# Scale of the context from a sum on TensorE, VectorE's side work moved behind the first score maxima: one change to a fused kernel of attention and experts

## The chip, the cores and the metric

The kernel runs on one core of a Trainium2 chip. A core has five engines that work side by side and meet through semaphores: TensorE (PE; its weight loads are shown as PEld), VectorE (DVE), ScalarE (ACT), GpSimd (POOL) and SyncE (SP), which here only issues DMAs. Each engine takes its instructions in the order in which the program lists them, so an instruction that waits holds back everything behind it on its engine. The metric is the device time of one execution in microseconds.

## The reference

For 64 batches of 256 rows with 1024 columns (`x`) and a context of 256 rows with 256 columns each, attention with 32 query heads on 8 key heads is added to `x`, and then a mixture of 8 experts, two for each row:

```python
x = x + attention(layernorm(x), ctx_512, ctx_512)       # 32 heads of 32, 8 key heads
x = x + experts(layernorm(x), router_w, w1, w2)         # top 2 of 8, inner width 704
# attention: softmax(q k^T / sqrt(32)) v, keys and values are both the context
# experts:   logits = x router_w^T; top 2; softmax of the two;
#            y = w2[e] (silu(gate) * up), gate and up from w1[e] x
```

All is in fp32; the kernel computes it with pairs of fp16 numbers, a high part and a low part, and for that scales each operand by a power of two that is found from its largest absolute value.

## The kernel before

The program has stages one after another: constants and the split of the weights into high and low parts (to 420 us), the stage `fuse` (to about 8730 us), and two stages that run the rest of the expert blocks of 512 and 256 rows. The change is in `fuse` alone.

`fuse` runs iterations i = 0 to 67. Iteration i loads batch i, scales and splits its context (iterations 0 to 63), computes score maxima for batch i - 1 and exponentials and values for the batches before it, adds attention to x and normalizes for batch i - 3, routes batch i - 4, and from i = 13 on it multiplies one block of 512 rows with an expert's weights. From iteration 14 on pairs of iterations are the body of a hardware loop, up to 61; every engine has its own copy of it and jumps back to its head every second iteration. An iteration has eight steps, k = 0 to 7, and a step four quarters, q = 0 to 3. In each step TensorE multiplies four score tiles (L704) and four tiles for the maxima (L721), adds up the values (L686 to L690), and between them, in 64 even pieces per iteration, the experts' products (L862, L883). This interleaving is written out by hand, in the `iteration` function of each engine; there is no planner.

What moves one step forward goes through all engines: the scores of L704 lie in one PSUM tile, `a_sc`. ScalarE reads it twice (L946 to `a_p` in fp32, L947 to `a_ph` in fp16). The fp16 rest `a_pl` = `a_p` - `a_ph` is made by GpSimd for the quarters 0 and 1 (L1172) and by VectorE for 2 and 3 (L1364). `a_p` has one buffer for each quarter, so ScalarE cannot write quarter 0 or 1 of the next step before GpSimd has read that of the last. VectorE divides the values (L1373, L1376, to `a_att`), and may write the next `a_att` when GpSimd has added the last to `a_xres` (L1145). VectorE's maxima of the scores (L1343) free the two halves of `a_mx` for TensorE.

The scale of the context: at step 0, VectorE takes the largest absolute value in each partition (`largest_ctx`, L1418, to `a_cmax`). GpSimd makes one maximum of the 128, in all partitions (`partition_all_reduce`, L1193, to `a_call`). At step 1 VectorE makes the power of two and its inverse from it (`scale_ctx`, L1424 to L1431), with which ScalarE and VectorE split the context into `a_ksrc`.

What stands around these in the order of each engine: on GpSimd the all-reduce stands between the subtraction of quarter 0 and that of quarter 1 in step 0, followed by the DMA that adds the experts' last rows to the output (`add_rows`, L1132). On VectorE step 0 begins with `largest_ctx` and `pick_block` (L1315 to L1334, eleven small instructions that choose the next block of rows and its expert), then come the copies of the turned queries (`q_out`, L1357), the first score maxima (`max_out`, L1343) and the attention output (`o_out`). In steps 1 and 2, the statistics of the next x (`stats_x`, L1396) stand ahead of these too. `a_mi` is one PSUM bank in which TensorE puts small things: the turned maxima (`turn_max`, L810), logits and counts.

Of the kernel before, what the change touches and what calls it, by code (L numbers as in the profile page):

```python
# [5 lines left out]
P = 128  # L6
# [12 lines left out]
D = 32  # L19
# [325 lines left out]
def fuse(nc, x, ctx_in, x1, xn_parts, slots, w1_parts, w2_parts, scales, router_parts, router_scale, ident,  # L345
# [29 lines left out]
    with ExitStack() as ctx:  # L375
        def sb(name, shape, dt):
            return ctx.enter_context(nc.sbuf_tensor(name, shape, dt))
# [26 lines left out]
        nb1, nb2 = sb("a_nb1", [P, 2], F32), sb("a_nb2", [P, 2], F32)  # L404
        cmax, call, cgrd = sb("a_cmax", [P, 1], F32), sb("a_call", [P, 1], F32), sb("a_cgrd", [P, 1], F32)
        cpow, crec, cinv = sb("a_cpow", [P, 1], F32), sb("a_crec", [P, 1], F32), sb("a_cinv", [P, 1], F32)
# [40 lines left out]
        LG = MI[:, 256:256 + 2 * E].rearrange("p (c e) -> p c e", c=2)  # L447
        CN = MI[:, 320:320 + 3 * E].rearrange("p (c e) -> p c e", c=3)
        Y = ps("e_y", [P, 2, BLOCK], F32)

# [217 lines left out]
        def _(pe):  # L668
            pe.wait_ge(filled, 2)
            pe.wait_ge(rows_cleared, 3)  # L670
# [109 lines left out]
            def turn_rows(i, g):  # L780
# [16 lines left out]
                last.then_inc(turned, 1)  # L797

            def turn_max(i, k):
                b, p = mtu(i, k - 1)  # L800
                if k % 2 == 0 or not on(b):
                    return
                pe.wait_ge(n["maxed"], b * 32 + 8 * (p + 1))
                at_least(pe, n["max_low"], b * 4 + p)
                if k == 5 and on(i - 4):
                    pe.wait_ge(n["route"], (i - 4) * ROUTE + 1)
                if k == 7 and on(i - 4):
                    pe.wait_ge(n["route"], (i - 4) * ROUTE + COUNTS_READ)
                for c in range(2):
                    last = pe.transpose(MI[0:2 * G, c * P:(c + 1) * P], nmax[:, c, 8 * p:8 * p + 8], ident[:, :])  # L810
                last.then_inc(n["max_turned"], 1)
# [88 lines left out]
            def iteration(i, par, fused):  # L900
                for k in range(8):
# [14 lines left out]
                    max_score(i, k, par, 2)  # L916
                    turn_max(i, k)
                    values(i, k, par)
                    experts(i, 8 * k + 5, par, fused)
# [11 lines left out]
        def _(act):  # L931
            act.wait_ge(filled, 2)

# [158 lines left out]
        def _(pool):  # L1092
            pool.memset(xg[:, :, :].rearrange("p a b -> p (a b)").bitcast(U32), 0).then_inc(xg_cleared, 1)
            pool.memset(ksrc[:, :, :, 3 * D:3 * D + 2], 1.0).then_inc(filled, 1)
            pool.memset(ksrc[:, :, :, 3 * D + 2:P], 0.0).then_inc(filled, 1)
# [88 lines left out]
            def iteration(i, par, fused):  # L1184
                m, m1 = i - LAG, i - LAG + 1
                now, soon, before = live(m, fused), live(m1, fused), live(m - 1, fused)
                for k in range(8):
                    low_p(i, k, 0)
                    if k == 0 and on(i):
                        pool.wait_ge(n["ctx_max"], i + 1)  # L1190
                        at_least(pool, n["ctx_chain"], i * 4)
                        settle(pool, passed)
                        pool.partition_all_reduce(call[:, :], cmax[:, :], P, RMAX).then_inc(n["ctx_all"], 1)  # L1193
                    if k == 0 and before:
# [39 lines left out]
        def _(dve):  # L1234
# [186 lines left out]
            def scale_ctx(i):  # L1421
                dve.wait_ge(n["ctx_all"], i + 1)
                at_least(dve, n["k_low"], i)
                dve.tensor_scalar(cgrd[:, :], call[:, :], 1e-30, None, ALU.max).then_inc(n["ctx_chain"], 1)  # L1424
                dve.wait_ge(n["ctx_chain"], i * 4 + 1)
                dve.tensor_single_scalar(cpow[:, :].bitcast(I32), cgrd[:, :].bitcast(I32), EXPONENT,
                                         ALU.bitwise_and).then_inc(n["ctx_chain"], 1)
                dve.wait_ge(n["ctx_chain"], i * 4 + 2)
                dve.reciprocal(crec[:, :], cpow[:, :]).then_inc(n["ctx_chain"], 1)
                dve.wait_ge(n["ctx_chain"], i * 4 + 3)  # L1430
                dve.tensor_scalar(cinv[:, :], crec[:, :], 8.0, None, ALU.mult).then_inc(n["ctx_chain"], 1)  # L1431

# [9 lines left out]
            def scale_exps(i, par):  # L1442
                at_least(dve, n["exps"], (i - 1) * 32)
                dve.tensor_scalar(escale[:, par:par + 1], cpow[:, :], 0.125 / float(D) ** 0.5, None,
                                  ALU.mult).then_inc(n["escaled"], 1)

            def scale_values(i, par):
                dve.tensor_scalar(vscale[:, par:par + 1], cpow[:, :], 0.125, None, ALU.mult).then_inc(n["vscaled"], 1)

# [81 lines left out]
            def iteration(i, par, fused):  # L1531
                for k in range(8):
                    if k == 0 and on(i):
                        largest_ctx(i, par)
                    if k == 0 and live(i - LAG + 1, fused):
                        pick_block(i - LAG + 1, par)
                    if k in (1, 2) and on(i):
                        stats_x(i, k - 1)
                    q_out(i, k)
                    if k == 1 and on(i - 3):  # L1540
                        spread_x1(i - 3)
                    experts(i, 8 * k, par, fused)
                    max_out(i, k, 0)
                    o_out(i, k, par)
                    if k == 5 and on(i - 4):
# [512 lines left out]
```

## Time and profile before

| | us |
|---|---|
| median of three executions | 10104.24 (10095.11 to 10106.83) |
| the profiled execution | 10093.03 |
| its span, first to last instruction | 10091.3 |
| mean granted clock of TensorE | 0.913 |
| TensorE busy | 8676.8 (86%) |
| VectorE busy | 6024.0 (60%) |
| ScalarE busy | 4560.9 (45%) |
| GpSimd busy | 3786.1 (38%) |

The profile is of one execution. Its waits view sums, for each engine, tile and line, the idle time just before an instruction, by the instruction that released it; "issue" as the releaser means that no semaphore is seen to have held it. A windows row gives, for a stretch in us, its length, then busy time and count of instructions of PE, PEld, DVE, ACT and POOL, the granted clock of TensorE as a share of full speed (1.00 is 2.4 GHz, 0.50 is 1.2 GHz), the share of DMA and GB/s. A timeline row has start, length, engine, line, operation, tiles, shapes, count, and in brackets the idle time before it with its releaser. The row of a line gives the least, median and largest duration in ns.

### The profile page before, as it was taken

Reading aid. Unit: us, or ns where it says so; the run is one execution under the profiler, and the core shown is the slowest. Engines: PE = TensorE matmul, PEld = TensorE weight load, DVE = VectorE, ACT = ScalarE, POOL = GpSimd, SP = SyncE. Lnnn points to the kernel's source line nnn. Section 1 sums busy time; section 2 is a strip of 40 time slices with the busy share of each in tenths; the row PEclk is TensorE's granted clock in tenths of the full one; section 3 lists DMA queues with packets and bytes.
Section 4 is the critical chain, followed back from the end, with each engine's and each line's share of the span. In section 5 each row is a group of like instructions: output and inputs, shape, how many; then the busy total and the mean of one; then the engine's idle time right before and its main releaser. Section 6 shows DMA issues by size and latency. Waiting matters only on the chain. (4 is left out here: it accounts for less than half of the span.)

```text
span 10091.3 us, 212936 instructions
## 1 busy us (share of the span) xinstructions
PE 8676.8 (86%) x73448; PEld 4865.3 (48%) x73448; DVE 6024.0 (60%) x11995; ACT 4560.9 (45%) x6962; POOL 3786.1 (38%) x5045
## 2 busy tenths in 40 slices
PE   4455569999898999999999899999989989989989
PEld 3333335544444555555455445545545545444457
DVE  7877776666666666666666666666666666222212
ACT  3466654554544555554455544445554445200001
POOL 0145544444444444444444444444444444211111
PEclk7656569999999999999999999999999999999999
DMA  9742124444444444444444444444444444454444
GB/s 366 299 167 96 46 86 137 132 126 128 127 135 131 135 124 134 129 131 135 131 137 123 131 123 136 136 133 132 125 129 128 135 131 138 124 191 146 157 168 165
DMA packets 455392, 1434.12 MB, mean 142 GB/s; under 512 B 90088, under 2 KB 110568, under 8 KB 454128
## 3 DMA queue, kind: packets, MB, share of 16 engines
q1 hardware_dynamic: 360240, 1132.12, 33.3%
q0 software_dynamic: 94016, 287.65, 12.2%
q8 instruction: 615, 10.08, 0.4%
q14 instruction: 521, 4.27, 0.1%
HBM read 1034.41 MB, written 408.21 MB: 143 GB/s over the span
## 5 line engine op out<-in xcount | busy, mean ns | idle before, releaser
L862 PE MATMUL e_y<-e_xt,e_w 128*128 128x512 f16 x14520 | 3601.7, 387 | 0.0
L946 ACT ACTIVATE a_p<-a_sc,a_escale 128x512 f32<-128x512 f32 x2048 | 1407.1, 687 | 3026.2 <-PE a_sc L704 2202.4
L1172 POOL TENSOR_TENSOR a_pl<-a_p,a_ph 128x512 f16<-128x512 f32 x1024 | 1232.9, 1204 | 3008.2 <-ACT a_ph L947 2429.9
L1343 DVE TENSOR_REDUCE a_nmax<-a_mx 128x2 f32<-128x512 f32 x2048 | 1404.9, 687 | 1218.2 <-PE a_mx L721 1201.8
L862 PEld LDWEIGHTS e_y<-e_xt,e_w 128*128 128x128 f16 x14520 | 1391.2, 99 | 1412.0 <-issue 96.7
L883 PE MATMUL e_y<-e_w,e_yt 128*128 128x512 f16 x7480 | 1863.6, 379 | 41.1 <-DVE e_yt L1506 41.1
L704 PE MATMUL a_sc<-a_qs,a_ks 128*128 128x512 f16 x2048 | 854.6, 417 | 845.0 <-ACT a_ph L947 817.1
L947 ACT ACTIVATE a_ph<-a_sc,a_escale 128x512 f16<-128x512 f32 x2048 | 1395.2, 681 | 0.0
L883 PEld LDWEIGHTS e_y<-e_w,e_yt 128*128 128x128 f16 x7480 | 695.4, 97 | 697.3 <-issue 65.0
L721 PE MATMUL a_mx<-a_ks,a_qs 96*128 96x256 f16 x4096 | 865.9, 296 | 143.2 <-DVE a_nmax L1343 139.1
L704 PEld LDWEIGHTS a_sc<-a_qs,a_ks 128*128 128x128 f16 x2048 | 203.7, 99 | 1178.4 <-ACT a_ph L947 866.5
L1364 DVE TENSOR_TENSOR a_pl<-a_p,a_ph 128x512 f16<-128x512 f32 x1024 | 758.3, 741 | 14.4 <-ACT a_ph L947 14.2
L1357 DVE COPY a_qs<-a_tr 64x1024 f16<-64x1024 f16 (+1 forms) x1024 | 701.5, 685 | 59.9 <-PE a_tr L743 47.4
L721 PEld LDWEIGHTS a_mx<-a_ks,a_qs 96*128 96x128 f16 x4096 | 413.4, 104 | 625.9 <-DVE a_nmax L1343 169.7
L686 PE MATMUL a_pv<-a_v,a_ph 128*128 128x34 f16 x8192 | 693.0, 182 | 6.9 <-DVE a_att L1376 4.4
L690 PE MATMUL a_pv<-a_v,a_pl 128*128 128x34 f16 x8192 | 687.1, 181 | 0.0
L688 PE MATMUL a_pv<-a_v,a_ph 128*128 128x32 f16 x8192 | 686.7, 180 | 0.0
L686 PEld LDWEIGHTS a_pv<-a_v,a_ph 128*128 128x128 f16 x8192 | 658.4, 99 | 48.1 <-DVE a_att L1376 23.5
L688 PEld LDWEIGHTS a_pv<-a_v,a_ph 128*128 128x128 f16 x8192 | 650.5, 99 | 10.4
L690 PEld LDWEIGHTS a_pv<-a_v,a_pl 128*128 128x128 f16 x8192 | 645.1, 99 | 0.0
L1036 ACT ACTIVATE e_rows<-e_y,e_gate 128x512 f32<-128x512 f32 x440 | 302.4, 687 | 587.3 <-PE e_y L883 420.9
L1145 POOL TENSOR_TENSOR a_xres<-a_att,a_xres 128x128 f32<-128x128 f32 x1024 | 524.9, 563 | 38.7 <-DVE a_att L1376 36.2
(236 smaller groups left out, 11485.3 us busy)
## 6 DMA issues: line engine op xcount, KB each, us to landing
e_w<-w_parts SPq DMA_DIRECT2D x935, 512.0 KB, 3.5
f_w<-w_parts SPq DMA_DIRECT2D x153, 512.0 KB, 5.2
w_parts<-w_parts SPq DMA_DIRECT2D x136, 512.0 KB, 4.9
h_w<-w_parts SPq DMA_DIRECT2D x136, 512.0 KB, 6.1
a_x<-in_x SPq DMA_DIRECT2D x64, 1024.0 KB, 4.9
a_xres<-in_x SPq DMA_DIRECT2D x64, 1024.0 KB, 8.1
out<-a_xres SPq DMA_DIRECT2D x64, 1024.0 KB, 7.7
xn_parts<-a_xhl SPq DMA_DIRECT2D x64, 1024.0 KB, 10.0
```

Source lines behind the costliest of these rows:

```text
L686: pe.matmul(PV[:, c, g, 0:D + 2], PH[:, kv % 2, g // 2, tt, cols], V1[:, vp, tt, kv, 0:D + 2], start=tt == 0, stop=False)
L688: pe.matmul(PV[:, c, g, 0:D], PH[:, kv % 2, g // 2, tt, cols], V1[:, vp, tt, kv, D + 2:2 * D + 2], start=False, stop=False)
L690: last = pe.matmul(PV[:, c, g, 0:D + 2], PL[:, kv % 2, g // 2, tt, cols], V1[:, vp, tt, kv, 0:D + 2], start=False, stop=tt == 1)
L704: pe.matmul(SC[:, :], KS[:, sp_, kv, tt * P:(tt + 1) * P], QS[:, kv, half * 2 * S:(half + 1) * 2 * S], start=True, stop=True).then_inc(n[" ...
L721: last = pe.matmul(MX[:, q % 2, g2, :], QS[0:96, kv, g * S + half * P:g * S + half * P + P], KS[0:96, mp, kv, :], start=True, stop=True)
L862: last = pe.matmul(Y[:, bank, :], w1r[:, t % RING, h, pw, :], xT[:, px, h, :], start=r == 0, stop=r == 3 * HT - 1)
L883: last = pe.matmul(Y[:, bank, :], yT[:, py, t, c * P:(c + 1) * P], w2b[:, t, pw, half * (H // 2):(half + 1) * (H // 2)], start=r == 0, sto ...
L946: act.activation(PF[:, q, :], SC[:, :], ACT.Exp, scale=escale[:, sp_:sp_ + 1])
L947: act.activation(PH[:, kv % 2, h, tt, :], SC[:, :], ACT.Exp, scale=escale[:, sp_:sp_ + 1]).then_inc(n["exps"], 1)
L1172: pool.tensor_tensor(PL[:, kv % 2, q // 2, q % 2, :], PF[:, q, :], PH[:, kv % 2, q // 2, q % 2, :], ALU.subtract).then_inc(n["p_low"], 1)
L1343: dve.reduce_max(nmax[:, half, kv * G + 2 * gp:kv * G + 2 * gp + 2], MX[:, q % 2, :, :], AX.X, negate=True).then_inc(n["maxed"], 1)
L1364: dve.tensor_tensor(PL[:, kv % 2, q // 2, q % 2, :], PF[:, q, :], PH[:, kv % 2, q // 2, q % 2, :], ALU.subtract).then_inc(p_low2, 1)
```

## The change

The maximum over partitions becomes a sum over partitions: TensorE multiplies a matrix of ones in fp32 with the column of the 128 maxima (`sum_ctx`), in step 0 behind the third pair of matmuls for the score maxima and ahead of the values. The sum, in all 128 partitions, lies in one column of `a_mi`, from which `scale_ctx` reads it. The sum is between 1 and 128 times the largest value, so the constants change: 1024 in place of 8, and 2^-10 in place of 0.125. The matrix of ones is written once by GpSimd at the stage's start. The turn of the maxima in step 1, which writes to the same PSUM bank, waits until the sum has been read. On VectorE, `q_out`, the experts' instructions of the step's first piece, `max_out` of quarter 0 and `o_out` now come ahead of `largest_ctx`, `pick_block` and `stats_x`.

```diff
         CN = MI[:, 320:320 + 3 * E].rearrange("p (c e) -> p c e", c=3)
+        CS = MI[:, 352:353]
...
+            def sum_ctx(i):
+                if not on(i):
+                    return
+                pe.wait_ge(n["ctx_max"], i + 1)
+                at_least(pe, n["max_low"], (i - 2) * 4 + 3)
+                pe.matmul(CS, ones[:, :], cmax[:, :], start=True, stop=True).then_inc(n["ctx_all"], 1)
+
             def turn_max(i, k):
                 b, p = mtu(i, k - 1)
                 if k % 2 == 0 or not on(b):
                     return
+                if k == 1 and on(i):
+                    pe.wait_ge(n["ctx_chain"], i * 4 + 1)
...
                     turn_max(i, k)
+                    if k == 0:
+                        sum_ctx(i)
                     values(i, k, par)
...
                     low_p(i, k, 0)
-                    if k == 0 and on(i):
-                        pool.wait_ge(n["ctx_max"], i + 1)
-                        at_least(pool, n["ctx_chain"], i * 4)
-                        settle(pool, passed)
-                        pool.partition_all_reduce(call[:, :], cmax[:, :], P, RMAX).then_inc(n["ctx_all"], 1)
                     if k == 0 and before:
                         add_rows(m - 1, par, 3)
...
-                dve.tensor_scalar(cgrd[:, :], call[:, :], 1e-30, None, ALU.max).then_inc(n["ctx_chain"], 1)
+                dve.tensor_scalar(cgrd[:, :], CS, 1e-30, None, ALU.max).then_inc(n["ctx_chain"], 1)
...
                 for k in range(8):
+                    q_out(i, k)
+                    if k == 1 and on(i - 3):
+                        spread_x1(i - 3)
+                    experts(i, 8 * k, par, fused)
+                    max_out(i, k, 0)
+                    o_out(i, k, par)
                     if k == 0 and on(i):
                         largest_ctx(i, par)
                     if k == 0 and live(i - LAG + 1, fused):
                         pick_block(i - LAG + 1, par)
                     if k in (1, 2) and on(i):
                         stats_x(i, k - 1)
-                    q_out(i, k)
-                    if k == 1 and on(i - 3):
-                        spread_x1(i - 3)
-                    experts(i, 8 * k, par, fused)
-                    max_out(i, k, 0)
-                    o_out(i, k, par)
```

GpSimd in the loop, at the turn from step 0's first subtraction to its second (`a_pl`); the ISA rows without a tile at L1193 and L1172 are those that the trace shows as MODIFY_POOL_CONFIG. Before:

```order
L1172 TENSOR_TENSOR a_pl<-a_p,a_ph 128x512 [waits a_exps]
L1190 REGISTER_ALU
L32 REGISTER_ALU [waits a_ctx_max]
L1193 ISA [waits a_ctx_chain]
L1193 ISA a_call<-a_cmax 128x1
L1126 REGISTER_ALU
L1132 DMA out<-e_rows,e_idx 16384x1024 [waits e_weighed]
L1171 REGISTER_ALU
L1172 ISA
L1172 TENSOR_TENSOR a_pl<-a_p,a_ph 128x512 [waits a_exps]
L1142 REGISTER_ALU
L1145 TENSOR_TENSOR a_xres<-a_att,a_xres 128x128 [waits a_o_done]
```

After:

```order
L1185 TENSOR_TENSOR a_pl<-a_p,a_ph 128x512 [waits a_exps]
L1139 REGISTER_ALU
L1145 DMA out<-e_rows,e_idx 16384x1024 [waits e_weighed]
L1184 REGISTER_ALU
L1185 TENSOR_TENSOR a_pl<-a_p,a_ph 128x512 [waits a_exps]
L1155 REGISTER_ALU
L1158 TENSOR_TENSOR a_xres<-a_att,a_xres 128x128 [waits a_o_done]
```

The reduction and the two MODIFY_POOL_CONFIG rows are gone; between the subtractions stands only the DMA that adds rows.

VectorE in the loop, from the last routing instruction of the iteration (`tok`) into step 0. Before:

```order
L1307 TENSOR_SCALAR tok<-tok 128x2 [waits a_route]
L1418 TENSOR_REDUCE a_cmax<-a_ctx 128x1 [waits a_ctx_all,ctx_in1]
L1312 REGISTER_ALU
L32 ISA [waits a_route]
L1315 TENSOR_TENSOR e_left<-next_slot,taken 128x8 [waits e_y1_there,e_picked]
...
L1334 CAST e_blk<-e_spot 128x1 [waits e_picked]
L1357 COPY a_qs<-a_tr 64x4x256 [waits a_scores,a_q_turned]
L1357 COPY a_qs<-a_tr 32x4x256
L1357 COPY a_qs<-a_tr 64x4x256
L1357 COPY a_qs<-a_tr 32x4x256
L1340 REGISTER_ALU
L1343 TENSOR_REDUCE a_nmax<-a_mx 128x2 [waits a_max_turned,a_max_scores]
```

After:

```order
L1315 TENSOR_SCALAR tok<-tok 128x2 [waits a_route]
L1365 COPY a_qs<-a_tr 64x4x256 [waits a_scores,a_q_turned]
L1365 COPY a_qs<-a_tr 32x4x256
L1365 COPY a_qs<-a_tr 64x4x256
L1365 COPY a_qs<-a_tr 32x4x256
L1348 REGISTER_ALU
L1351 TENSOR_REDUCE a_nmax<-a_mx 128x2 [waits a_max_turned,a_max_scores]
L1379 REGISTER_ALU
L32 REGISTER_ALU [waits a_pv]
L1381 RECIPROCAL a_orec<-a_pv 128x8 [waits a_x1_done]
L1384 SCALAR_TENSOR_TENSOR a_att<-a_pv,a_vscale,a_orec 128x256 [waits a_vscaled,a_o_recip]
L1426 TENSOR_REDUCE a_cmax<-a_ctx 128x1 [waits a_ctx_all,ctx_in1]
...
L1323 TENSOR_TENSOR e_left<-next_slot,taken 128x8 [waits e_y1_there,e_picked]
```

The copies to `a_qs`, the maxima `a_nmax` and the output `a_att` have moved ahead of the context's maximum and of the picking of a block, which begins with `e_left`.

TensorE in the loop, step 0, from the third pair of matmuls for the maxima to the values (`a_pv`), after the change:

```order
L722 MATMUL a_mx<-a_ks,a_qs 128x256 [waits a_maxed]
L722 MATMUL a_mx<-a_ks,a_qs 128x256
L803 REGISTER_ALU
L32 REGISTER_ALU [waits a_ctx_max]
L805 MATMUL a_mi<-a_cmax,a_ones 128x1 [waits a_max_low]
L679 ISA
L32 ISA [waits a_v_made,a_p_low2,a_p_low]
L687 MATMUL a_pv<-a_v,a_ph 128x34 [waits a_o_done]
L689 MATMUL a_pv<-a_v,a_ph 128x32
```

The matmul of L805 and its waits are new, ahead of the values; the other rows stand as before.

## Rows read from the trace of the kernel before

**Rows 1.** Waits, 1736.72 to 8276.70: total us, times, longest us.

```profile
ACT a_p L946 <- POOL a_pl L1172: 590.8, 48, 17.0
DVE a_orec L1373 <- POOL a_xres L1145: 507.3, 48, 14.6
...
POOL a_pl L1172 <- issue: 475.4, 57, 10.9
PE a_sc L704 <- ACT a_ph L947: 449.3, 59, 13.9
...
POOL a_call L1193 <- issue: 338.3, 48, 9.0
...
DVE a_cmax L1418 <- issue: 114.7, 23, 6.0
...
PE a_mx L721 <- DVE a_nmax L1343: 81.5, 23, 4.1
```

**Rows 2.** Windows view of the same stretch.

```profile
1736.72:8276.70 6539.98, 5945.00 (x52082) 3294.36 (x52081) 4175.04 (x8593) 3294.64 (x4993) 2787.98 (x3696) 0.95 0.45 131
```

**Rows 3.** Windows view of one pair of iterations, in pieces.

```profile
5006.09:5025.70 19.61, 19.59 (x145) 10.14 (x143) 17.88 (x41) 8.76 (x14) 10.04 (x12) 1.00 0.86 240
5025.70:5037.90 12.20, 0.02 (x1) 0.02 (x2) 0.47 (x2) 1.26 (x2) 2.79 (x5) 0.65 0.43 86
5037.90:5043.20 5.30, 5.30 (x60) 3.08 (x61) 4.33 (x12) 1.89 (x3) 3.93 (x14) 0.51 0.03 6
5043.20:5146.90 103.70, 101.66 (x901) 56.79 (x898) 64.52 (x127) 58.02 (x88) 44.31 (x53) 1.00 0.44 132
...
5150.00:5153.10 3.10, 0.46 (x3) 0.00 (x0) 3.00 (x5) 1.51 (x3) 2.11 (x2) 1.00 1.06 191
5153.10:5168.50 15.40, 14.67 (x111) 7.59 (x111) 11.80 (x24) 4.76 (x7) 2.50 (x2) 0.89 0.57 123
5168.50:5174.40 5.90, 0.09 (x2) 0.07 (x2) 0.52 (x2) 1.26 (x2) 2.56 (x4) 0.86 0.28 90
5174.40:5179.70 5.30, 5.30 (x60) 3.04 (x61) 4.32 (x12) 1.89 (x3) 4.06 (x14) 0.51 0.00 0
```

**Rows 4.** Timeline of GpSimd in the same pair.

```profile
5014.50 1.75 POOL L1172 TENSOR_TENSOR a_pl<-a_p,a_ph 128x512 f16<-128x512 f32 x1
5023.61 0.38 POOL L1193 PARTITION_ALL_REDUCE a_call<-a_cmax  x1 [7.36 <-issue]
5024.19 1.80 POOL L1132 DMA_INDIRECT out<-e_rows,e_idx  x1 [0.20 <-issue]
5035.39 1.14 POOL L1172 TENSOR_TENSOR a_pl<-a_p,a_ph 128x512 f16<-128x512 f32 x1 [9.41 <-issue]
5036.50 0.85 POOL L1145 TENSOR_TENSOR a_xres<-a_att,a_xres 128x128 f32<-128x128 f32 x2
```

**Rows 5.** Line L1193 over the whole run.

```profile
L1193 POOLq MODIFY_POOL_CONFIG  x126: 1/10/629, 442.7 to 8286.5; - x126
```

**Rows 6.** Timeline of VectorE at the loop's head.

```profile
5146.90 0.69 DVE L1418 TENSOR_REDUCE a_cmax<-a_ctx 128x1 f32<-128x512 f32 x1 [4.83 <-issue]
...
5150.02 2.79 DVE L1357 COPY a_qs<-a_tr 64x1024 f16<-64x1024 f16 x4
5152.84 0.69 DVE L1343 TENSOR_REDUCE a_nmax<-a_mx 128x2 f32<-128x512 f32 x1
```

**Rows 7.** Timeline of ScalarE behind it.

```profile
5157.36 0.63 ACT L1025 ACTIVATE e_yt<-e_th 64x512 f16<-64x512 f32 x1 [5.83 <-DVE e_th L1487]
```

**Rows 8.** Line L810, 1736.72 to 8276.70.

```profile
L810 PE MATMUL a_mi<-ident,a_nmax x384: 269/273/422, 1771.8 to 8268.8; 128*8 128x128 f32 x192
```

**Rows 9.** Line L1506, the same stretch.

```profile
L1506 DVE TENSOR_TENSOR e_yt<-e_th,e_yt x240: 678/854/1990, 1771.3 to 8233.5; 128x512 f16<-128x512 f32 x120
```

**Rows 10.** Waits, 439.34 to 1471.98, before the experts start.

```profile
DVE a_orec L1373 <- POOL a_xres L1145: 97.2, 11, 11.6
...
DVE a_cmax L1418 <- DMA a_ctx<-in_ctx: 5.0, 1, 5.0
```

More of the change, by code:

```diff
@@ L404, in fuse @@
         nb1, nb2 = sb("a_nb1", [P, 2], F32), sb("a_nb2", [P, 2], F32)
-        cmax, call, cgrd = sb("a_cmax", [P, 1], F32), sb("a_call", [P, 1], F32), sb("a_cgrd", [P, 1], F32)
+        cmax, cgrd, ones = sb("a_cmax", [P, 1], F32), sb("a_cgrd", [P, 1], F32), sb("a_ones", [P, P], F32)
         cpow, crec, cinv = sb("a_cpow", [P, 1], F32), sb("a_crec", [P, 1], F32), sb("a_cinv", [P, 1], F32)
@@ L668, in _ @@
         def _(pe):
-            pe.wait_ge(filled, 2)
+            pe.wait_ge(filled, 3)
             pe.wait_ge(rows_cleared, 3)
@@ L931, in _ @@
         def _(act):
-            act.wait_ge(filled, 2)
+            act.wait_ge(filled, 3)
             def exps(i, k, par, q):
@@ L1093, in _ @@
             pool.memset(xg[:, :, :].rearrange("p a b -> p (a b)").bitcast(U32), 0).then_inc(xg_cleared, 1)
+            pool.memset(ones[:, :], 1.0).then_inc(filled, 1)
             pool.memset(ksrc[:, :, :, 3 * D:3 * D + 2], 1.0).then_inc(filled, 1)
@@ L1430, in scale_ctx @@
                 dve.wait_ge(n["ctx_chain"], i * 4 + 3)
-                dve.tensor_scalar(cinv[:, :], crec[:, :], 8.0, None, ALU.mult).then_inc(n["ctx_chain"], 1)
+                dve.tensor_scalar(cinv[:, :], crec[:, :], 1024.0, None, ALU.mult).then_inc(n["ctx_chain"], 1)
             def low_k(i, par):
@@ L1443, in scale_exps @@
                 at_least(dve, n["exps"], (i - 1) * 32)
-                dve.tensor_scalar(escale[:, par:par + 1], cpow[:, :], 0.125 / float(D) ** 0.5, None,
+                dve.tensor_scalar(escale[:, par:par + 1], cpow[:, :], 2.0 ** -10 / float(D) ** 0.5, None,
                                   ALU.mult).then_inc(n["escaled"], 1)
             def scale_values(i, par):
-                dve.tensor_scalar(vscale[:, par:par + 1], cpow[:, :], 0.125, None, ALU.mult).then_inc(n["vscaled"], 1)
+                dve.tensor_scalar(vscale[:, par:par + 1], cpow[:, :], 2.0 ** -10, None, ALU.mult).then_inc(n["vscaled"], 1)
             def stats_x1(b, par, c):
```

## The prediction

> **What bounds the kernel now.** I read the waits of the steady stretch first, 48 iterations (15 to 62) from 1736.72 to 8276.70 us [rows 1], then busy time and clock over one pair of iterations [rows 3], then GpSimd's timeline inside it [rows 4]. TensorE is the bound: 5945.00 us busy of 6539.98 [rows 2]. What it is not busy is almost one wait: 449.3 us before the scores of L704, for the exponentials of ScalarE [rows 1]. The reader is to follow that wait back. ScalarE itself waits 590.8 us for GpSimd's subtraction of L1172, exactly 48 times, once per iteration, and VectorE waits 507.3 us for GpSimd's addition of L1145, 48 times [rows 1]. And GpSimd waits for nobody: 338.3 us before L1193 and 475.4 us before L1172 stand under "issue", which means that no semaphore held it [rows 1].
>
> The timeline shows it once in full: the subtraction begins at 5014.50, takes 1.75, then 7.36 us of nothing, an all-reduce of 0.38, an issue of a DMA, 9.41 us of nothing, and only then the next subtraction at 5035.39 and the addition at 5036.50 [rows 4]. GpSimd's queue shows 126 MODIFY_POOL_CONFIG at the all-reduce's line [rows 5], two records for each of the 63 iterations after the first. So it is not the 0.38 us of reduction that costs, but that GpSimd is reconfigured to run it, and once more for the next subtraction. For that time the two buffers between ScalarE and GpSimd are full, then everyone stops: from 5025.70 to 5037.90 TensorE works 0.02 us, VectorE 0.47, ScalarE 1.26 [rows 3]. In the other iteration of the pair the same stop is 5.90 us long (5168.50 to 5174.40), since TensorE had lost time shortly before [rows 3].
>
> Two more losses hang on it. After each stop TensorE's granted clock is 0.51, the 1.2 GHz level, for 5.30 us [rows 3]. And at the loop's head, every second iteration, VectorE comes about 5 us late (114.7 us in 23 waits before L1418, under "issue" again [rows 1]): it then does the maximum of the context and picks the block (5146.90 to 5150.02), copies the queries (2.79 us) and reaches the first score maxima only at 5152.84 [rows 6]; TensorE waits for these, 81.5 us in 23 waits [rows 1], and the next stretch runs at a granted 0.89 [rows 3].
>
> **The all-reduce goes.** Both reconfigurations go with it: in the changed order none is left between GpSimd's subtraction and the next one. GpSimd's way from one subtraction to the next is then the DMA issue of 1.80 us [rows 4] and nothing else, about 2 us where 20.9 stood (5014.50 to 5035.39), so it ends before ScalarE's buffers are full. I let the whole wait of TensorE go: 449.3 / 48 = 9.36 us per iteration. It ran in 51 iterations at TensorE's pace (13 to 63): 51 x 9.36 = 477 us. That is an upper end only if another engine was late underneath; against this speaks the long stretch 5043.20 to 5146.90, where all engines run without one and TensorE is busy 101.66 of 103.70 us [rows 3]. Lower end: a fifth of it comes back as another wait, 380.
>
> **The clock after the stops.** 5.30 x (1 - 0.51) = 2.6 us of work lost per stop, at both places [rows 3]: 51 x 2.6 = 133 us. In the dense stretch, whose idle shares are small, the row shows 1.00 [rows 3], so I let all of it go; lower end 90, if some new wait lets the clock fall.
>
> The Trainium skill, GPSIMD Engine Reference, section 4.1 Engine selection, speaks against this change: it names GpSimd for a reduction over partitions. Its section 2.1 Instruction dispatch says that the first call of freshly loaded code pays about 6 us, with no visible instruction. The trace agrees with the second and gives more, 7.36 and 9.41 us [rows 4]; by the page's figure the two would be an estimated 12 us per iteration.
>
> **The sum on TensorE.** 64 matmuls of a 128 x 128 matrix of ones with one column, in fp32. No such matmul is in the trace; the nearest is the fp32 transpose of L810, 273 ns [rows 8], pipelined among others. Between 0.1 us (a single column where L810 has 128) and 1.0 (nearly four such rows one after another), I take 0.3, the nearest to that row: 51 x 0.3 = 15 us lost (5 to 51). It stands behind the third score maxima of step 0 and holds back the values and the experts' matmuls behind it. It waits for VectorE's maximum of the context, which in the iterations without a late loop head is done some 2 us before TensorE gets there, so nothing waits. The new wait in the turn of the maxima (step 1) costs nothing: VectorE's reading of the sum stands ahead of the score maxima that this turn waits for anyway.
>
> **VectorE's order at step 0.** The copies, the first maxima and the attention output come 3.1 us earlier (0.69 of context and the picking, 5146.90 to 5150.02 [rows 6]), in the iterations with a late loop head. There 2.64 us idle (5150.00 to 5153.10, 0.46 busy) and 15.40 x (1 - 0.89) = 1.7 of clock are to be had, 4.3 per pair [rows 3]. But what is next is close: the sum waits there for the context's maximum, some 4.8 us after 5146.90 (2.79 copies, 0.6 maxima, 0.7 output, 0.7 context), about 1 us after TensorE could go on; and ScalarE waits for VectorE's product until 5157.36 [rows 7], which the new order does not bring forward, as all the moved work still lies ahead of it, and holds back the next scores by about another 1 us. With 0.4 left of the wait itself, 1.5 us per pair remain (0 to 4.3): 25.5 x 1.5 = 38 us (0 to 110). The moved picking delays the load of the next block's slots by 4 us at most; the load also waits for GpSimd's row addition, issued at 5024.19 behind the all-reduce [rows 4], which now comes some 7 us earlier, so it costs nothing.
>
> **Before the experts start** (iterations 2 to 12) VectorE waits 97.2 us in 11 waits for the same addition of GpSimd [rows 10]; the engine is the busiest there. I take 90 (50 to 110).
>
> **The sum.** 477 + 133 - 15 + 38 + 90 = 723 us. From the profiled execution's 10093.03 that gives 9370; the median of three is 11 us above it (10104.24), so I forecast **9380 us**. The bounds of the terms give its own range: all gained, 477 + 133 - 5 + 110 + 110 = 825 and 9279; the low ends, 380 + 90 - 51 + 0 + 50 = 469 and 9635, though not all at once, so 9270 to 9470.
>
> **Rivals.** *The wait moves to VectorE.* GpSimd's subtraction and addition now run while VectorE is busy, where so far VectorE stood still beside them. The two slow each other: VectorE's subtraction of L1506 takes 678 ns at the least, 854 in the median and 1990 at the most [rows 9]. With four such meetings of 0.3 to 1 us in steps 0 and 1, where VectorE is busy 17.9 of 19.6 us (its row over 5006.09 to 5025.70 [rows 3]), VectorE comes up to 3.5 us late to the score maxima and TensorE waits: 51 x 3.5 = 180, so 9560 (9470 to 9650). Against it: the same meetings lie in the dense stretch, and TensorE loses 2 us of 103.70 there. The Trainium skill, SBUF — State Buffer, section Who interferes with whom, states this rule: a VectorE instruction with two inputs from SBUF and a GpSimd instruction that reads SBUF block each other in full; the spread of L1506 agrees.
>
> *TensorE waits in its own queue: slower.* Before, a late context held GpSimd and VectorE; now TensorE itself stands at the sum, with values and experts behind it. It becomes slower than before once that wait is over (477 + 133 - 15 + 38) / 51 = 12.4 us per iteration. With 16 us it would be 10104 - 90 + 51 x 3.6 = 10,200. It needs the context's load to come late; VectorE waited for that load once, 5.0 us, at the start [rows 10]. Little speaks for it.
>
> *The reconfigurations stay.* Were they demanded by something else than the all-reduce, the stops would stay and the sum's 15 us be added: 10,119, no change. The 126 records at the all-reduce's own line [rows 5] speak against it.
>
> **How the numbers follow.** Forecast 0.75, VectorE late 0.18, reconfigurations stay 0.03, slower 0.04. Some 0.03 of the first lies outside its range and the upper half of the second above 9540, so 9265 to 9540 holds about 8 in 10. A measurement of this kernel can tell 0.2% from no change, 20 us. Faster by more: 0.93; within: 0.03; slower: 0.04.
>
> **What would show it.** Right: no MODIFY_POOL_CONFIG between two subtractions after the first iterations; ScalarE's wait for L1172 and VectorE's for L1145 nearly gone; a pair of iterations near 248 us where 272.39 stood, with the granted clock at 0.98 or above. Wrong in size: a wait of TensorE for VectorE's score maxima above 3 us per iteration (first rival), or a wait before the sum itself (second). The order at step 0 is right if the waits for the first score maxima at the loop's head fall under 1 us each; if they vanish without another wait in their place, I was too low there.

## The result: the stops are gone, and 54 us more than forecast are left

| | before | after |
|---|---|---|
| median of the runs shown (us) | 10099.67 (10092.09 to 10106.83) | 9433.78 (9431.56 to 9438.21) |
| ratio after to before, 95% interval | | 0.9338 (0.9326 to 0.935) |
| profiled execution (us), its span | 10093.03, 10091.3 | 9433.45, 9431.7 |
| start of the span to the first maximum of the context | 420.3 | 422.2 |
| iterations 0 to 12 (the ramp) | 1051.7 | 953.1 |
| iterations 13 to 62 (TensorE's pace) | 6804.8 | 6261.4 |
| iteration 63 to the end | 1814.5 | 1794.9 |

The lower four rows are cut at the starts of VectorE's maximum of the context (L1418 before, L1426 after), one per iteration. The profiled run gained 659.6 us: 98.5 in the ramp, 543.4 in 50 iterations at TensorE's pace and 19.6 behind them, most of it the stop of iteration 63 (a wait of TensorE of 13.3 us before), less 1.9 ahead of the first maximum. Forecast were 9380, in a range of 9265 to 9540. One execution of the kernel of experiment 6 took 27391.19 us at a granted clock of 0.535, and the times and ratios here leave it out.

The waits of the steady stretch of after, 48 iterations as in [rows 1] (total us, times, longest us):

```profile
POOL a_pl L1185 <- ACT a_ph L959: 2289.6, 576, 9.0
...
PE a_mx L722 <- DVE a_nmax L1351: 59.3, 56, 3.5
...
PE e_y L893 <- DVE e_yt L1514: 38.7, 48, 0.8
...
PE a_sc L705 <- ACT a_ph L959: 37.3, 40, 1.3
...
PE a_mi L805 <- DVE a_cmax L1426: 16.3, 19, 0.9
...
ACT a_p L958 <- POOL a_pl L1185: 1.3, 1, 1.3
```

ScalarE's wait for GpSimd's subtraction went from 590.8 us to 1.3. VectorE's wait for GpSimd's addition, 507.3 us, has no row any more. GpSimd, which stood under "issue" for 475.4 us before its subtraction, now waits at that line for ScalarE, as an engine with slack does. What is left of TensorE's waits for other engines' work is small, and has a new order: VectorE's score maxima first, then VectorE's low part of the experts' product (L893, 38.7 us in 48 waits before the change too), then the exponentials, then, new, VectorE's maximum of the context before the sum (L805).

The windows view of the same stretch and of one pair of iterations inside it (stretch, us, then busy us and instructions of PE, PEld, DVE, ACT, POOL, granted clock, DMA share, GB/s):

```profile
1622.89:7636.79 6013.90, 5844.17 (x52178) 3260.89 (x52177) 4270.57 (x8593) 3287.08 (x4992) 2751.97 (x3649) 1.00 0.49 142
4761.00:5011.80 250.80, 243.27 (x2177) 135.63 (x2174) 177.63 (x359) 138.06 (x210) 115.03 (x154) 1.00 0.50 143
```

Against [rows 2], TensorE's idle time fell from 594.98 us to 169.73, and its busy time from 5945.00 to 5844.17 with the granted clock up from 0.95 to 1.00. So of 526.1 us gained in 48 iterations, 425.2 are idle time and 100.8 are busy time, which I read as the clock's gain less what the sum adds.

GpSimd's timeline at a loop head of after (start us, us, engine, line, operation), which answers to [rows 4]:

```profile
4760.61 1.76 POOL L1185 TENSOR_TENSOR a_pl<-a_p,a_ph 128x512 f16<-128x512 f32 x1
4762.54 1.58 POOL L1145 DMA_INDIRECT out<-e_rows,e_idx  x1 [0.17 <-issue]
4763.58 1.74 POOL L1185 TENSOR_TENSOR a_pl<-a_p,a_ph 128x512 f16<-128x512 f32 x1
4764.69 1.44 POOL L1158 TENSOR_TENSOR a_xres<-a_att,a_xres 128x128 f32<-128x128 f32 x2
```

From one subtraction to the next it is 2.97 us where 20.89 stood; both empty stretches are gone. The whole trace of after holds no MODIFY_POOL_CONFIG later than 414 us. Before, four records belonged to nearly every iteration: two at the all-reduce's line [rows 5], and two at the line of the subtraction behind it, on the way back:

```profile
L1172 POOLq MODIFY_POOL_CONFIG  x124: 82/615/615, 507.2 to 8297.7; - x124
```

VectorE at the same loop head, answering to [rows 6]:

```profile
4756.94 2.79 DVE L1365 COPY a_qs<-a_tr 64x1024 f16<-64x1024 f16 x4 [4.67 <-PE a_sc L705]
4759.76 0.69 DVE L1351 TENSOR_REDUCE a_nmax<-a_mx 128x2 f32<-128x512 f32 x1
...
4761.00 0.68 DVE L1426 TENSOR_REDUCE a_cmax<-a_ctx 128x1 f32<-128x512 f32 x1
4761.60 0.81 DVE L1323 TENSOR_TENSOR e_left<-next_slot,taken 128x8 f32<-128x8 f32 x1
...
4762.90 2.85 DVE L1329 TENSOR_TENSOR e_lpri<-e_lead,expert_order 128x8 f32<-128x8 f32 x1
...
4768.06 0.67 DVE L1351 TENSOR_REDUCE a_nmax<-a_mx 128x2 f32<-128x512 f32 x1
```

and TensorE's three waits there:

```profile
4761.81 0.38 PE L805 MATMUL a_mi<-a_cmax,a_ones 128*128 128x1 f32 x2 [0.58 <-DVE a_cmax L1426]
...
4768.80 0.39 PE L722 MATMUL a_mx<-a_ks,a_qs 96*128 96x256 f16 x2 [1.98 <-DVE a_nmax L1351]
...
4771.99 0.39 PE L705 MATMUL a_sc<-a_qs,a_ks 128*128 128x512 f16 x1 [1.29 <-ACT a_ph L959]
```

The third is the wait for ScalarE, which itself stands for VectorE's product, as in [rows 7]:

```profile
4770.15 0.63 ACT L1037 ACTIVATE e_yt<-e_th 64x512 f16<-64x512 f32 x1 [8.07 <-DVE e_th L1495]
```

VectorE still comes 4.67 us late to the loop's head. The first maxima are now only 2.82 us behind that, and TensorE doesn't wait for them here. But the maximum of the context and the picking stand between the first and the second maxima, and an operation on 128 x 8 numbers (L1329) takes 2.85 us there, beside GpSimd's subtraction and addition of the fence above. The second maxima are at 4768.06, and TensorE waits 1.98 us for them.

### The profile page after: what moved, and what is told of

It is laid out like the page before. It is cut to its first block and busy times, and to the rows that moved or that the text cites. A ratio compares the mean times of both kernels' runs of the same rounds, so it can differ in the third digit from the quotient of the medians.

```text
span 9431.7 us, 212875 instructions
## 1 busy us (share of the span) xinstructions
PE 8575.2 (91%) x73576; PEld 4834.2 (51%) x73576; DVE 6136.2 (65%) x11995; ACT 4553.3 (48%) x6962; POOL 3743.7 (40%) x4982
## 5 line engine op out<-in xcount | busy, mean ns | idle before, releaser
L872 PE MATMUL e_y<-e_xt,e_w 128*128 128x512 f16 x14520 | 3519.6, 380 | 0.1
L1185 POOL TENSOR_TENSOR a_pl<-a_p,a_ph 128x512 f16<-128x512 f32 x1024 | 1283.5, 1254 | 2753.4 <-ACT a_ph L959 2753.4
L872 PEld LDWEIGHTS e_y<-e_xt,e_w 128*128 128x128 f16 x14520 | 1373.5, 98 | 1368.9 <-issue 13.9
L893 PE MATMUL e_y<-e_w,e_yt 128*128 128x512 f16 x7480 | 1863.2, 379 | 41.2 <-DVE e_yt L1514 41.2
L893 PEld LDWEIGHTS e_y<-e_w,e_yt 128*128 128x128 f16 x7480 | 695.3, 97 | 697.7 <-issue 65.0
L722 PE MATMUL a_mx<-a_ks,a_qs 96*128 96x256 f16 x4096 | 853.1, 292 | 106.8 <-DVE a_nmax L1351 105.2
L722 PEld LDWEIGHTS a_mx<-a_ks,a_qs 96*128 96x128 f16 x4096 | 402.9, 103 | 584.9 <-DVE a_nmax L1351 159.4
L687 PEld LDWEIGHTS a_pv<-a_v,a_ph 128*128 128x128 f16 x8192 | 653.9, 98 | 26.9 <-DVE a_att L1384 4.8
L1158 POOL TENSOR_TENSOR a_xres<-a_att,a_xres 128x128 f32<-128x128 f32 x1024 | 560.9, 627 | 21.7 <-DVE a_att L1384 19.5
```

Source lines behind the costliest of these rows:

```text
L687: pe.matmul(PV[:, c, g, 0:D + 2], PH[:, kv % 2, g // 2, tt, cols], V1[:, vp, tt, kv, 0:D + 2], start=tt == 0, stop=False)
L722: last = pe.matmul(MX[:, q % 2, g2, :], QS[0:96, kv, g * S + half * P:g * S + half * P + P], KS[0:96, mp, kv, :], start=True, stop=True)
L872: last = pe.matmul(Y[:, bank, :], w1r[:, t % RING, h, pw, :], xT[:, px, h, :], start=r == 0, stop=r == 3 * HT - 1)
L893: last = pe.matmul(Y[:, bank, :], yT[:, py, t, c * P:(c + 1) * P], w2b[:, t, pw, half * (H // 2):(half + 1) * (H // 2)], start=r == 0, sto ...
L1185: pool.tensor_tensor(PL[:, kv % 2, q // 2, q % 2, :], PF[:, q, :], PH[:, kv % 2, q // 2, q % 2, :], ALU.subtract).then_inc(n["p_low"], 1)
```

## The experiments

Eleven runs on three chips, each beside runs of the kernel before on its own chip (medians 10083.43, 10088.15, 10088.73), so ratios are compared. The waits quoted are those of iterations 15 to 62 of each kernel. Kernel 1 is that of experiment 1, and so on; "after" is the changed kernel.

**1. The sum alone.** The changed kernel, with VectorE's old order at step 0:

```diff
                 for k in range(8):
+                    if k == 0 and on(i):
+                        largest_ctx(i, par)
+                    if k == 0 and live(i - LAG + 1, fused):
+                        pick_block(i - LAG + 1, par)
+                    if k in (1, 2) and on(i):
+                        stats_x(i, k - 1)
                     q_out(i, k)
...
                     o_out(i, k, par)
-                    if k == 0 and on(i):
...
```

> The sum on TensorE stands as in the changed kernel; VectorE's order at step 0 is that of the kernel before (context maximum and picking of a block ahead of the query copies and the first score maxima). Prediction's own price of the order, 38 us: then this kernel takes 9434 + 38 = 9472 us, and TensorE's wait for the first score maxima at the loop's head is back at 2 to 3 us. Rival, that the moved picking collides with GpSimd's subtraction and loses what the order gains: 9434 within 20 us, with the picking (first to last of its small instructions) back from 4.1 us in the mean to about 2.1.

Measured: 9404.36, ratio 0.9327 (0.9312 to 0.9343), not slower than the whole change (0.9338), where the prediction's price would have made it 38 us slower. TensorE's waits:

```profile
PE a_mx L722 <- DVE a_nmax L1351: 87.3, 47, 6.6
...
PE a_sc L705 <- ACT a_ph L959: 11.0, 21, 1.2
```

The wait for the first maxima is back as in [rows 1] (81.5 before, 87.3 here), but the 16.3 us before the sum are gone and the one before the scores fell from 37.3 to 11.0. The new order moves waits about, and is worth nothing that these runs can tell: the whole gain is that of the sum in the all-reduce's place. The time is that of the rival, and the picking is back at 2.38 us on average.

**2. The order alone.** The kernel before, with the changed order of VectorE's step 0 (the diff of 1 turned round).

> The kernel before with VectorE's new order alone; the all-reduce stays on GpSimd. If the stops come from GpSimd's reconfiguration for the all-reduce, they stay whole: 126 MODIFY_POOL_CONFIG at that line, VectorE's wait for GpSimd's addition near 500 us in 48 waits, and the time 10,100 within 50 (the order may win up to 38, or move into the stop). If the order itself had removed the stops, some 9500.

Measured: 10066.58, ratio 0.9981 (0.9972 to 0.9991).

```profile
ACT a_p L946 <- POOL a_pl L1172: 620.0, 48, 17.0
...
PE a_sc L704 <- ACT a_ph L947: 520.8, 82, 14.0
...
PE a_mx L721 <- DVE a_nmax L1343: 19.9, 36, 1.0
```

The order does what it is for: the wait for maxima falls from 81.5 us to 19.9. But the wait for the exponentials, behind GpSimd's stop, rises from 449.3 to 520.8. In waits, whatever is gained ahead of the stop is waited away in it. What did come through, 17 us of the time (0.2%), stands in TensorE's busy time, 5911.24 us in 48 iterations where 5945.00 stood. The stops are whole, as expected.

**3. GpSimd without the reconfiguration.** The kernel before in the new order, its all-reduce replaced by an ordinary operation of GpSimd, with nothing on TensorE. The kernel leaves out the maximum over partitions; TensorE has the same work, 52083 matmuls in the 48 iterations where [rows 2] has 52082:

```diff
-                        pool.partition_all_reduce(call[:, :], cmax[:, :], P, RMAX).then_inc(n["ctx_all"], 1)
+                        pool.tensor_copy(call[:, :], cmax[:, :]).then_inc(n["ctx_all"], 1)
```

> The new VectorE order, no sum on TensorE, and on GpSimd a copy of the 128 maxima in place of the all-reduce at the same place: it leaves out the maximum over partitions, so each partition gets a scale of its own. It tells the reconfiguration from the wait for the context's maximum on GpSimd's queue. If the reconfiguration is all of the stop: at or below the changed kernel, 9434 less the sum's 0.67 us per iteration (34 us), 9400. If GpSimd's wait for VectorE's maximum were part of it: above 9500, with ScalarE waiting for GpSimd's subtraction in 48 waits as before.

Measured: 9430.18, ratio 0.9351 (0.9335 to 0.9366), the same as the whole change, and so not the 34 us less that were expected.

```profile
PE a_mx L721 <- DVE a_nmax L1343: 93.4, 66, 4.0
...
ACT a_p L946 <- POOL a_pl L1172: 2.5, 2, 1.3
...
POOL a_call L1193 <- DVE a_cmax L1418: 1.2, 2, 0.7
```

GpSimd's place in the chain, its wait for VectorE's maximum and its operation between two subtractions are all still there, and the stops are gone all the same (590.8 to 2.5). So the stop was not that GpSimd has work there, but that it was switched. It also shows that, in the time of the kernel, the sum on TensorE costs no more than a copy on GpSimd does: without it the wait for the maxima is 93.4 us where 59.3 stand.

**4. The all-reduce twice.** The kernel before, with a second reduction in front of the first, into a column that nobody reads:

```diff
+                        pool.partition_all_reduce(call2[:, :], cmax[:, :], P, RMAX)
                         pool.partition_all_reduce(call[:, :], cmax[:, :], P, RMAX).then_inc(n["ctx_all"], 1)
```

> The kernel before with GpSimd's all-reduce issued twice in a row, the first into a column that nobody reads. Theory A (the stop is paid per switch of GpSimd from its ordinary operations to the reduction and back, once each way however many reductions lie between): the two empty stretches of 7.4 and 9.4 us stay as they are, and only the second reduction comes in addition, 0.4 to 2 us: 51 x 0.4 to 2 = 20 to 100 us more than before, 10,100 to 10,190. Rival (each reduction pays for itself, 16.8 us): the stop grows by 16.8 us per iteration, 51 x 16.8 = 857 us more, about 10,940.

Measured: 10102.74, ratio 1.0015 (1.0006 to 1.0024), so 15 us more, 0.3 per iteration. GpSimd's timeline:

```profile
5030.38 0.38 POOL L1194 PARTITION_ALL_REDUCE a_call<-a_cmax  x1 [6.83 <-issue]
5030.67 0.42 POOL L1195 PARTITION_ALL_REDUCE a_call<-a_cmax  x1
5031.28 1.80 POOL L1133 DMA_INDIRECT out<-e_rows,e_idx  x1 [0.19 <-issue]
5042.71 1.14 POOL L1173 TENSOR_TENSOR a_pl<-a_p,a_ph 128x512 f16<-128x512 f32 x1 [9.62 <-issue]
```

One empty stretch ahead of both reductions, none between them, one behind: the price is per switch, once each way, and the reduction itself is nearly free. The records say the same: the first reduction's line has as many MODIFY_POOL_CONFIG as [rows 5], the second's (L1195) has none.

```profile
L1194 POOLq MODIFY_POOL_CONFIG  x126: 1/320/631, 441.9 to 8299.4; - x126
```

The rival, each reduction paying its own 16.8 us, would have given 10,940.

**5. The picking behind the last maxima of step 0.** The changed kernel; the next block is picked at the end of step 0:

```diff
-                    if k == 0 and live(i - LAG + 1, fused):
-                        pick_block(i - LAG + 1, par)
...
                     max_out(i, k, 3)
                     low_p(i, k, 3)
+                    if k == 0 and live(i - LAG + 1, fused):
+                        pick_block(i - LAG + 1, par)
```

> The changed kernel with the picking of a block moved once more, behind the last score maxima of step 0. Theory: the waits left to TensorE in step 0 (59 us for score maxima, 37 us for the scores behind ScalarE, over 48 iterations) come from the picking, stretched from 2.1 to 4.1 us by GpSimd's subtraction, ahead of the second maxima and of the first expert product; then they fall by more than half and the time is 9340 to 9390. Rival: they come from VectorE's late start at the loop's head alone, and the time stays at 9434 within 20.

Measured: 9408.84, ratio 0.9329 (0.9313 to 0.9344); the interval overlaps that of the whole change. Neither expectation came whole: the waits in step 0 fell as the theory has it, and the time did not follow.

```profile
PE a_mi L820 <- DVE a_cpow L1434: 36.3, 35, 1.0
PE a_mi L805 <- DVE a_cmax L1426: 17.6, 20, 0.9
PE a_sc L705 <- ACT a_ph L959: 13.2, 23, 1.3
PE e_y L872 <- DVE e_th L1498: 11.1, 27, 1.8
...
PE a_mx L722 <- DVE a_nmax L1351: 7.1, 12, 1.8
```

The wait for the maxima fell from 59.3 to 7.1 and that for the exponentials from 37.3 to 13.2. A new one of 11.1 came up before the experts' product (L872), and one of 36.3 in step 1: the turn of the maxima (L820) shares a PSUM bank with the sum and waits until VectorE has read it (the scaling, L1432 to L1439), and that now stood right behind the picking.

**6. The sum later, and 7. the picking in step 1.** Beside the changed kernel itself, once more. In 6 the sum stands behind the fourth score maxima; 7 is 6 with the picking at the end of step 1, behind the scaling:

```diff
                     max_score(i, k, par, 2)
                     turn_max(i, k)
-                    if k == 0:
-                        sum_ctx(i)
...
                     max_score(i, k, par, 3)
+                    if k == 0:
+                        sum_ctx(i)
```

```diff
                     max_out(i, k, 3)
                     low_p(i, k, 3)
+                    if k == 1 and live(i - LAG + 1, fused):
+                        pick_block(i - LAG + 1, par)
```

> The changed kernel itself, unedited, once more, beside the next two on the same chip, since they are to be told apart by less than 1%. Every theory expects the ratio to the kernel before that it had, 0.9338 (0.9326 to 0.935): about 9420 us.

> The changed kernel with the sum on TensorE behind the fourth score maxima of step 0 in place of the third, so some 3 us later in TensorE's queue. Theory A (the sum comes too early for VectorE's maximum of the context, and this wait is a loss of its own, 0.66 us before L805 in every second iteration, and 0.5 us of waits behind it): the waits before the sum vanish and nothing takes their place, 20 to 35 us less than the changed kernel. Theory B (VectorE is behind in step 0 whatever TensorE does first, so that a wait taken away there comes back at the next thing VectorE makes): the wait before the sum goes, those before the score maxima, the scores or the turn of the maxima grow by as much; within 0.2% of the changed kernel.

> As the run before, and besides VectorE picks the next block at the end of step 1 in place of step 0, so a step later than in the run that picked behind the last maxima of step 0, and behind the scaling of the context, for which TensorE's turn of the maxima waits. Theory A (VectorE's lateness in step 0 is the sum of the work put there, and in step 1 there is room for it): the waits before the maxima and the scores at the loop's head (2.9 us in one iteration, 1.9 in the other) fall under 0.5 each without a new one; 51 x 1.9 = 97 us less than the changed kernel, about 9320. Theory B (the work is late wherever it is put near the loop's head, as the collisions with GpSimd go with it): less than half of that, above 9370; the wait stands before the scores or the turn of the maxima of step 1 or 2.

Measured: the changed kernel 9433.29, ratio 0.9349 (0.9337 to 0.9361); the later sum 9446.23, 0.9386 (0.9354 to 0.9418), no gain (four of its runs lie at 9439 to 9448, and one at 9543.58 widens the interval); the picking in step 1 9315.68, **0.9231** (0.9219 to 0.9243), 118 us less than the changed kernel, where theory A had 97. TensorE's waits with the later sum alone:

```profile
PE a_mx L722 <- DVE a_nmax L1351: 91.7, 62, 4.4
...
PE a_sc L705 <- ACT a_ph L959: 15.6, 23, 1.1
```

and with the picking in step 1:

```profile
PE a_sc L705 <- ACT a_ph L959: 21.9, 34, 1.5
PE a_mx L722 <- DVE a_nmax L1351: 10.2, 15, 2.2
...
PE a_mi L820 <- DVE a_cpow L1434: 2.1, 2, 1.0
```

With the later sum the wait before it (16.3) is gone and the one before the scores is 22 us shorter, but the one for the maxima has grown by 32: theory B for the sum. With the picking in step 1, the waits for maxima, scores and turn are 34 us together where 113 stand in after (59.3 + 37.3 + 16.3, the last for the sum), and nothing takes their place: theory A for the picking, though the waits that are left are still 0.6 us each on average, and not under the 0.5 it gave as its sign. Of the 102.8 us that kernel 7 gains on after in the 48 iterations (5911.08 against 6013.90), 26.9 are TensorE's busy time (5817.31 against 5844.17), the rest its idle time.

**8. What of kernel 7 does it.** The same kernel again, then with the sum where the change had put it, then with the maximum of the context and the statistics ahead of the copies as before the change (the picking in step 1 in all three).

> The kernel with the later sum and the picking in step 1, unedited, once more, beside the next two on the same chip. Every theory expects its ratio of 0.9231 (0.9219 to 0.9243), about 9315 us.

> The changed kernel with the picking at the end of step 1 and the sum where the change put it, behind the third score maxima. Theory A (the picking in step 0 is all of the lateness that was left; it is lengthened there by GpSimd's two-input operations that run beside it, 4.11 us where 1.88 stand in step 1): the wait before the sum stays, 0.3 us per iteration, and everything else goes as with the later sum: 9315 + 51 x 0.3 = 9330, at most 9340. Rival (the sum's place is a part of the gain, though alone it gave none): 9370 or more, with waits before the sum and the maxima.

> The picking at the end of step 1 and the later sum, but the maximum of the context (0.69 us) and the statistics of x ahead of the copies, maxima and output, as the kernel before has them. Theory A (the order of VectorE's side work only matters through the picking): within 0.2% of 9315. Rival (each us ahead of the first maxima at the loop's head is paid by TensorE): the maximum of the context costs 0.69 us in 25 iterations, the statistics of x (1.3 us) in steps 1 and 2 of all 51 if TensorE waits there: 9315 + 17 to 9315 + 17 + 66, so 9330 to 9400, with waits before L722 of 0.7 us per loop head or more.

Measured: 9317.48, ratio 0.9236 (0.9223 to 0.9249); with the early sum 9327.83, 0.9247 (0.9234 to 0.9259); with the old order 9326.56, 0.9245 (0.9232 to 0.9257). The three lie within 10 us, where the runs can hardly tell them apart. With the early sum, TensorE's waits show where its 10 us would be, as forecast (51 x 0.3 = 15):

```profile
PE a_mi L805 <- DVE a_cmax L1426: 17.7, 22, 0.9
...
PE a_mx L722 <- DVE a_nmax L1351: 9.1, 15, 1.9
```

With the old order, the wait for the maxima is somewhat longer than kernel 7's 10.2, and the time is within theory A's 0.2%:

```profile
PE a_mx L722 <- DVE a_nmax L1351: 16.6, 21, 2.0
```

So the picking's place is nearly all of it: after and the kernel with the early sum differ by that alone, 0.9338 (0.9349 when run again) and 0.9247, so 92 to 103 us of the 118. Kernel 1 and the last one here differ only by that and by the sum's place: 0.9327 and 0.9245, 83 us, or 1.6 per iteration, for 11 operations on 8 columns that take 2.38 us on average in kernel 1.

**Why the picking is dear in step 0.** Three of its lines, the first two in after, the third in kernel 7 (count: ns at the least, in the median, at the most):

```profile
L1329 DVE TENSOR_TENSOR e_lpri<-e_lead,expert_order x48: 166/314/2866, 1624.8 to 7516.5; 128x8 f32<-128x8 f32 x48
```

```profile
L1331 DVE TENSOR_REDUCE e_top<-e_lpri x48: 160/161/163, 1625.1 to 7516.8; 128x1 f32<-128x8 f32 x48
```

```profile
L1329 DVE TENSOR_TENSOR e_lpri<-e_lead,expert_order x48: 166/166/168, 1632.5 to 7422.0; 128x8 f32<-128x8 f32 x48
```

I laid each of these instructions over GpSimd's: of the 48 products of L1329 in after, 45 run beside an operation of GpSimd and each of them is longer than 166 ns, by 1.39 us on average; three run alone, longer by 0.03. The reduction of L1331, which reads one input, runs beside one 44 times and never takes more than 163. In kernel 7 none of the 48 meets one. The whole picking takes 2.13 us on average before, 4.11 in after, 1.88 in kernel 7. The Trainium skill, SBUF — State Buffer, section Who interferes with whom, says this of the two: VectorE's instructions with two inputs from SBUF contend with GpSimd's reads, a reduction never does; the rows agree.

But the lengthening alone isn't the loss. In kernel 5 the picking takes 2.51 us on average, and L1329 never more than 169 ns, and the time is near that of after; and in kernel 7, where the picking doesn't meet GpSimd, others do, at the loop's head:

```profile
4692.38 3.01 DVE L1495 SCALAR_TENSOR_TENSOR e_th<-e_th 64x512 f32<-64x512 f32 x1
...
4697.33 0.39 PE L705 MATMUL a_sc<-a_qs,a_ks 128*128 128x512 f16 x1 [1.40 <-ACT a_ph L959]
```

The experts' product takes 3.01 us there, 0.68 in the loop head of after. That lengthening still costs: ScalarE waits for this product, and TensorE waits 1.40 us for the scores behind it. But the second maxima come in time, where after has a wait of 1.98 us for them as well. I read kernels 1, 5 and 7 so: what counts is how much VectorE has to do, stretched or not, between the late loop head and the scaling that TensorE's turn needs; in step 1 behind the scaling there is room for 1.9 us more, in step 0 there is not. How the 118 us divide between the picking's own 1.9 us and its stretching wasn't tried apart.

## The prediction, step by step

**The stops (477 us): right, a tenth too high.** That the reconfigurations are all of the stop, and that GpSimd then hands over its subtraction in time, is shown by 3 and 4 and by the wait of 1.3 us. The wait for the exponentials fell from 449.3 to 37.3, by 412 in 48 iterations, so 438 in 51. The prediction let the whole wait go, and held that it would fail only where another engine underneath was late. One was: about two thirds of the 37.3 us stand at the loop's head, as the 1.29 us on TensorE's timeline do, which ScalarE's 8.07 us behind VectorE's late product make.

**The clock (133) and the sum's own time (15): right in size.** Together 118, so 111 for 48 iterations; TensorE's busy time fell by 100.8. The sum itself was in no row before; now it is (line L805 over the whole run, then the windows view of that line alone in the 48 iterations, PE and PEld):

```profile
L805 PE MATMUL a_mi<-a_cmax,a_ones x128: 168/250/374, 423.0 to 7639.6; 128*128 128x1 f32 x128
```

```profile
1622.89:7636.79 6013.90, 15.59 (x96) 14.35 (x96) 1.00 0.49 142
```

Two records per iteration, the pair on the timeline 0.38 us, 15.59 us in 48 iterations where 14 were forecast: the 0.3 were well taken from the nearest row. With that added back to the 100.8, the clock gave 116.4 where 125 were forecast. In the iterations without a late loop head nothing waits before it, as forecast: all of the 16.3 us, 19 waits of 0.9, lie at loop heads, where the step on VectorE's order had put about 1 us.

**VectorE's order at step 0 (38): wrong.** It is worth nothing that the runs can tell beside the sum (1), and 17 us beside the stops, which ate the wait that it took away (2). Its figures don't come to its 1.5 us per pair either: 4.3 less 1, 1 and 0.4 leave 1.9, so 48 us, still further off. By its own sign it was right: the waits for the first maxima at the loop's head were to fall under 1 us each, and there are 9 of them in 23 loop heads, 5.4 us together. What failed is the look at what is next. The step found two waits that come next, the sum's and the scores', each of about 1 us, and both are there. It missed a third, the second score maxima, which in after stand behind the picking: 1.98 us on the timeline, and 44 of the 59.3 us before L722 in all. It had taken the picking at its length of before, within 3.1 us for the maximum of the context and the picking; in the new place these are 5.8 us (4761.00 to 4766.82), and the picking alone takes 4.11 us on average where 2.13 stood. The length alone isn't it, as kernel 5 shows: the step had no term for the place of the picking, ahead of the second maxima and the experts' product, and behind the scaling in step 1 the same eleven operations gained some 100 us.

**The ramp (90): right.** 98.5 us measured, and of the 97.2 us of VectorE's wait [rows 10] no row is left.

**The rivals.** *The wait moves to VectorE* was named with the right mechanism and partly happened: the collisions do lie in step 0, on the picking. Its price, 3.5 us per iteration, was some three times what stands there: TensorE's wait for the maxima is 59.3 / 48 = 1.2 us per iteration, below the 3 us which the prediction had set as its sign. *TensorE waits in its own queue* has its sign, the wait before the sum, at 0.3 us per iteration where 12.4 would have decided. *The reconfigurations stay* fell with the first profile.

**The sum.** For 48 iterations the prediction comes to 633 x 48 / 51 = 596 us; 526.1 came. Of the 70 missing, 37 are the exponentials' wait that stayed, 30 the order (36 forecast; the score maxima gave 22.2 and the wait before the sum took 16.3), 10 the clock and the sum's own time; smaller waits gave some 7 back. A pair takes 250.80 us where 248 were named. The large terms, the stops and the clock, each came a tenth short or less, with the mechanism forecast for them; that the order's term was wrong did not matter to the total, as it is 38 of 723. The two misses of size, the exponentials' wait and the order, are mostly one: behind a wait of 9.4 us, the prediction costed VectorE at the loop's head by the waits nearest to it and by its durations of before, where the place of the work and, in part, its new durations decide.

## What to carry to other kernels

An engine that stands under "issue" on both sides of one short special operation may be being switched; an ordinary operation in its place (3) and the special one twice (4) tell. Here the price is the two empty stretches, per switch and not per operation, so either take the operation off that engine, or put all such operations together. When the big wait goes, look at the engine that is second on that path, and move out of its busiest stretch whatever nobody waits for soon, to behind the last thing there that another engine needs; here 11 small operations in the wrong step cost some 100 us. A small two-input operation of VectorE must not be costed by its size where GpSimd works beside it.

## What the runs showed of the chip that I had not expected

A second all-reduce of GpSimd right behind the first costs 0.3 us in the time of an iteration, where the switch costs 6.8 us ahead of the first and 9.6 behind the last, with no instruction in its timeline for either (kernel 4). VectorE's product of 128 x 8 numbers took up to 2.87 us beside GpSimd's two-input operations, seventeen times its 0.166 alone. An fp32 matmul with one column shows as two records of 250 ns in the median, and took 0.38 us as a pair on the timeline.
